# Row maxima sent by GpSimd's own DMA queue instead of SyncE's, and 80 unread products added on TensorE

## The reference, cut to what matters

```python
x = x + tanh(g_xattn[0]) * L0_xattn(layernorm(x), ctx, ...)      # context attention, 77 context rows
x = x + tanh(g_ffn[0])   * L0_ffn(layernorm(x), wg, w1, b1, w2, b2)
x = x + tanh(g_xattn[1]) * L1_xattn(layernorm(x), ctx, ...)
x = x + tanh(g_ffn[1])   * L1_ffn(layernorm(x), ...)

def L0_ffn(x, wg, w1, b1, w2, b2):      # 8 experts, the best 2 of each row, capacity 256
    scores = softmax(x @ wg); topv, topi = top_k(scores, 2)
    ...                                  # rows sent to experts, relu(x @ w1 + b1) @ w2 + b2, gathered
def L1_xattn(x, img, ...):               # first part: self-attention, 16 heads of 8
    q = heads(nx @ W_sq + b_sq); k = heads(nx @ W_sk + b_sk); v = heads(nx @ W_sv + b_sv)
    s = einsum('bhqd,bhkd->bhqk', q, k) * SCALE
    so = merge(einsum('bhqk,bhkd->bhqd', softmax(s), v)) @ W_so + b_so
    ...                                  # then cross-attention and a gelu network
```

## Time and profile before

| | |
|---|---|
| median of 3 runs | 457.8 us (456.64 to 464.91) |
| the profiled execution's own time | 453.76 us |
| its span, first to last instruction | 452.0 us |
| TensorE busy | 349.2 us, 77% of the span |
| VectorE, ScalarE, GpSimd busy | 261.5, 201.8, 114.1 us |
| mean granted clock of TensorE | 0.89 |

### The profile page before, as it was taken

How to read it: one execution, slowest core, us unless ns; L and a number is a source line. 1 busy time by engine, 2 the same in 40 slices (tenths; PEclk the granted TensorE clock), 3 DMA queues, 4 the chain that set the end, 5 groups by cost and what they waited for, 6 DMA issues and landing times.

```text
span 452.0 us, 6689 instructions
## 1 busy us (share of the span) xinstructions
PE 349.2 (77%) x2487; PEld 208.2 (46%) x2487; DVE 261.5 (58%) x661; ACT 201.8 (45%) x317; POOL 114.1 (25%) x155
## 2 busy tenths in 40 slices
PE   1897500998089899999999799987972899988980
PEld 0676400897043422333323376554562443677860
DVE  5435500233379988888830687536369937773435
ACT  2321300322050777667787488564723435664210
POOL 2000178155140618111110000010000055562232
PEclk9998555899569999999999899998885899899986
DMA  4599112111306765100000000003999367431222
GB/s 113 149 190 326 55 52 78 50 35 40 116 24 172 192 168 122 29 3 2 3 1 1 0 0 1 2 0 122 392 305 290 128 203 235 144 98 36 62 78 52
DMA packets 35877, 46.01 MB, mean 102 GB/s; under 512 B 4779, under 2 KB 21683, under 8 KB 35845
## 3 DMA queue, kind: packets, MB, share of 16 engines
q1 hardware_dynamic: 33156, 38.57, 30.0%
q0 software_dynamic: 2688, 7.02, 5.5%
HBM read 31.67 MB, written 13.78 MB: 101 GB/s over the span
## 4 chain that ended last, share of the span: by engine, by line
PE 55%; DVE 13%; issue 9%; DMA 8%; ACT 7%; POOL 6%; SPq 1%; POOLq 0%; DVEq 0%; ACTq 0%
PE ps L1413 9%; PE ps L1620 6%; PE ps L1606 6%; PE ps L1581 5%; PE ps L1589 3%; DMA R<-h_d,srow 3%; PE ps L1722 3%; PE ps L1531 3%; POOL disp_d L541 2%; PE ps L1877 2%; PE ps L1770 2%; PE ps L1543 2%; PE ps L1731 2%; POOL y_d L554 1%; PE ps L1906 1%
## 5 line engine op out<-in xcount | busy, mean ns | idle before, releaser
L1222 DVE TENSOR_REDUCE early<-ps 128x1 f32<-128x512 f32 x128 | 81.3, 684 | 9.7 <-PE ps L1581 6.4
L758 ACT ACTIVATE R<-ps 128x1024 f32<-128x1024 f32 x64 | 62.5, 1020 | 19.8 <-PE ps L1606 18.9
L1413 PE MATMUL ps<-ident,R 128*77 128x128 f32 (+1 forms) x224 | 35.4, 296 | 31.9 <-DMA R<-disp_d 24.8
L1413 PEld LDWEIGHTS ps<-ident,R 128*77 128x77 f32 (+1 forms) x224 | 26.6, 152 | 50.5 <-DMA R<-disp_d 25.2
L1581 PE MATMUL ps<-R 72*128 72x512 bf16 x112 | 38.1, 381 | 0.9 <-DVE early L1222 0.8
L1606 PE MATMUL ps<-R 75*128 75x512 bf16 x128 | 37.6, 379 | 1.1 <-DMA R<-R 0.8
L624 POOL DMA_INDIRECT R<-h_d,srow x16 | 16.3, 1021 | 78.2 <-DMA h_d<-ff 71.2
L1620 PE MATMUL ps<-R,vaug 128*9 128x512 f32 x256 | 33.5, 595 | 0.6 <-ACT R L758 0.6
L1188 DVE TENSOR_SCALAR R<-ps,vcol 128x256 f32<-128x256 f32 x16 | 7.0, 479 | 38.0 <-PE ps L1531 38.0
L1581 PEld LDWEIGHTS ps<-R 72*128 72x128 bf16 x112 | 10.8, 96 | 31.5 <-DVE early L1222 20.9
L541 POOL DMA_INDIRECT disp_d<-R,srow x16 | 15.9, 993 | 37.2 <-DVE srow L1134 32.7
(11 more groups left out here) (324 smaller groups left out, 688.4 us busy)
## 6 DMA issues: line engine op xcount, KB each, us to landing
R<-in_L_ffn_W_dram SPq DMA_DIRECT2D x1, 6144.0 KB, 19.7
h_d<-R SPq DMA_DIRECT2D x12, 256.0 KB, 2.8
q_d<-R SPq DMA_DIRECT2D x24, 96.0 KB, 1.9
R<-k_d SPq DMA_DIRECT2D x24, 96.0 KB
R<-q_d SPq DMA_DIRECT2D x8, 288.0 KB
R<-in_L_ffn_w_dram SPq DMA_DIRECT2D x1, 2048.0 KB, 16.3
h_d<-ff SPq DMA_DIRECT2D x6, 256.0 KB, 2.4
disp_d<-R SPq DMA_DIRECT2D x1, 1032.0 KB, 12.2
```

Of the source, the lines that this page charges most:

```text
L758: s.activation(probs[idx % 4], ps[:, 2 * (idx % 2):2 * (idx % 2) + 2, :].rearrange("p b t -> p (b t)"), ACT.Exp, scale=QK_SCALE).then_inc( ...
L1222: v.tensor_reduce(mcol[:, u, col:col + 1], bank(ring_bank("row", n)), AX.X, ALU.max).then_inc(s1_max, 1)
L1413: return m.transpose(dst, src, ident[0:k, 0:k])
```

## The change

SyncE no longer sends the maxima. GpSimd waits for its own split of unit `u` and issues the three transfers itself, as part of its loop over the units, ahead of whatever it does next. TensorE gets 12 products of 512 columns ahead of the transposes of the first routing, 64 ahead of the transposes of sequence 0, and 4 between these and sequence 0's projections. All go to PSUM bank 1, which is free at these places, and wait for nothing.

```diff
-            def load_max(u):
-
-                b, hg = u // HG, u % HG
-                sp.wait_ge(max_parts, u + 1)
-                if u >= 2:
-                    sp.wait_ge(ld_max[u % 2], 16 * 3 * (u // 2))
-                for i in range(3):
-                    sp.dma_start(Q9[KQ + i:KQ + 1 + i, b, 4 * hg:4 * hg + 4, :].rearrange("p h (t q) -> p (h t) q", q=P),
-                                 mparts[:, u, i, :]).then_inc(ld_max[u % 2], 16)
-
...
             load_packed(0, 2)
-            load_max(0)
             load_packed(0, 3)
...
-            load_max(1)
             load_packed(1, 0)
             load_packed(1, 1)
-            load_max(2)
             load_packed(1, 2)
             load_packed(1, 3)
-            for u in range(3, UNITS):
-                load_max(u)
...
                 g.tensor_tensor(mparts[:, u, 2, :], mneg[:, :], mparts[:, u, 1, :], ALU.subtract).then_inc(max_parts, 1)
+                pool.wait_ge(max_parts, u + 1)
+                if u >= 2:
+                    pool.wait_ge(ld_max[u % 2], 16 * 3 * (u // 2))
+                b, hg = u // HG, u % HG
+                for i in range(3):
+                    g.dma_start(Q9[KQ + i:KQ + 1 + i, b, 4 * hg:4 * hg + 4, :].rearrange("p h (t q) -> p (h t) q", q=P),
+                                mparts[:, u, i, :]).then_inc(ld_max[u % 2], 16)
                 if u == 0:
                     pool.wait_ge(qk_ready, K_1)
...
+            def spin(columns):
+
+                m.matmul(ps[:, 1, 0:columns], ones_b[:, :], zeros[:, 0:columns // 2].bitcast(BF16), start=True, stop=True)
+
...
+            for i in range(12):
+                spin(512)
             transpose_tiles(sent[0][:, :, 0:D], ln_out, T, ln_tp)
...
-            def spin(columns):
-
-                m.matmul(ps[:, 1, 0:columns], ones_b[:, :], zeros[:, 0:columns // 2].bitcast(BF16), start=True, stop=True)
-
+            for i in range(64):
+                spin(512)
             transpose_tiles(xn, ln_out, 2 * T, ln_tp, [0])
+            for i in range(4):
+                spin(512)
             project_heads(0, 0)
```

More of the change, by code:

```diff
@@ L458, in _ @@
             sp.wait_ge(q_parts, 2)
-            for hg in range(HG):
-                store_queries(1, hg)
-            load_max(1)
+            store_queries(1, 0)
+            store_queries(1, 1)
+            store_queries(1, 2)
+            store_queries(1, 3)
             load_packed(1, 0)
             load_packed(1, 1)
-            load_max(2)
             load_packed(1, 2)
             load_packed(1, 3)
-            for u in range(3, UNITS):
-                load_max(u)
             sp.wait_ge(o_norm, 4 * HG)
```

## The result

Over 21 runs of each kernel the median is 462.5 us with the change and 459.7 us before. The ratio is 1.0091, with a 95% interval of 1.0058 to 1.0124: under 2%, but a small loss all the same, 4.2 us (2.7 to 5.7). It leaves out every execution over 1.5% above the fastest of its kernel, so it is not the quotient of the two medians (1.006). The same kernel run again beside three others gave 1.0092 (1.0034 to 1.0149). The forecast was 0.7 us more.

What follows compares the result with a forecast made beforehand. TensorE bounds steady loop steps; its clock falls at the routing and sequence 0. The sum 453.76 - 1.8 - 0.9 + 3.4 = 454.5 us, 0.7 more, became 458.5 on the runs' median; own range 456.5 to 460, wide 453 to 465.

Steps and rivals of the forecast that it cites:

- 1.8 forecast: First routing: 12 products hold the clock through transposes and logits, so the first scatter comes 1.8 us earlier; bounds 0 to 2.3.
- its reserve: Sequence 0: the masked copy of Q waits on VectorE's variances at 129.89 us, so 1.07 us at best arrives.
- 0.3 gained for 0.9: Sequence 0: the 64 + 4 products were forecast to bring the first scores 0.9 us earlier.
- Three take 3 x 0.98 + 2 x 0.30 = 3.54 us: Attention loop: GpSimd's time to issue a unit's three transfers, 3.54 us, taken from its indirect transfers.
- The waits forecast for units 3 and 7: Attention loop: late maxima cost 1.3 us in unit 3 and 1.6 us in unit 7.
- the rival of cheap transfers: Attention loop: direct transfers cost GpSimd 0.6 to 0.9 us each, landing in 3.2 to 4.2; time 455.1 to 456; chance 0.30.
- Three ... land 4.77 us after the parts: Attention loop: each unit's maxima land 4.77 us after GpSimd's parts, against 5.26 us available in a steady step.
- named contention only as a bound: Attention loop: contention or a longer form appears only in the upper bound, 6.3 us to landing.
- taken as 3.18 us from unit 7: Attention loop: SyncE's way, from its start at 232.64 to the wait's end at 235.82 in unit 7, at most 3.18 us.
- The term was +3.4 us: Attention loop: moving transfers to GpSimd adds 3.4 us of waits, 0.5 + 1.3 + 1.6; 0 by SyncE's bound, 13 by the upper.
- waits in every unit: Rival, attention loop: maxima land 6.2 us after parts, steady units wait 0.94 us each, 13.4 together; time 468.5; chance 0.12.
- the wide range: Whole kernel: 453 to 465 us, the top set half way to the case of waits in all units.

Runs made afterwards that it cites:

- pool_only: The changed kernel without any unread products, maxima still sent by GpSimd; ratio to the kernel before 1.0126 (1.0072 to 1.0180).
- pool_guard2: The changed kernel, all products, with SyncE's packed loads held until the maxima of units 0, 1 and 2 land; ratio to before 0.9939 (0.9893 to 0.9986).
- guard2_bare: The changed kernel without unread products, SyncE's packed loads held behind the maxima of units 0, 1 and 2; ratio to before 0.9936 (0.9891 to 0.9980).
- after_again: The changed kernel itself, unaltered, run again for a comparison beside three others and a second trace; ratio to before 1.0092 (1.0034 to 1.0149).
- split_units: The changed kernel, but SyncE sends the maxima of units 0 and 1, GpSimd those of 2 to 7; ratio to before 1.0079 (1.0038 to 1.0120).
- pool_warm: The changed kernel plus 24 unread products, 16 ahead of unit 0's wait and 8 ahead of unit 1's; ratio to before 1.0033 (0.9987 to 1.0079).
- guard3: The changed kernel, packed loads held behind units 0, 1 and 2, load (0,2) too waiting for unit 0's maxima; ratio to before 0.9995 (0.9954 to 1.0036).
- sp_spins: The changed kernel with all products, but the maxima given back to SyncE at their old places; ratio to before 1.0004 (0.9964 to 1.0044).
- guard2_64: The changed kernel with only the 64 + 4 products, packed loads held behind units 0, 1 and 2; ratio to before 0.9992 (0.9949 to 1.0035).

## Why the time lay in the stated range and the steps did not hold

- **12 products.** The clock held at 42 to 44 us and the first scatter came 1.4 us earlier, for 1.8 forecast. The passes of the logits did not all run at full clock: in this trace it fell at about 44.4 (0.61 from 44 to 46), and L1480 took 2.83 us, not 1.9. The rule of the Trainium skill that was weighed here ("TensorE: Matmul & The Clock Gate", Part 4: transposes don't count as busy for the clock as other products do) fits this trace; in the first trace of the changed kernel L1480 took 1.90 us, at full clock, behind the same transposes, so it did not decide in every execution. Of the ten traces with the 12 products five have 1.90 us, one 2.2 and four 2.7 to 2.8.
- **64 + 4 products.** The forecast's rows were right (L1560 in 1.98 us), its reserve was too: the masked copy waits for VectorE's variance. But that variance slipped. GpSimd's split of K (L546) also started earlier, and beside it VectorE's 128x4 operation took 0.98 us in place of 0.17 a few microseconds before. From the first transpose to the first scores: 7.12 us before, 6.82 after, 0.3 gained for 0.9.
- **GpSimd's time for the transfers.** "Three take 3 x 0.98 + 2 x 0.30 = 3.54 us", from indirect rows: measured 1.48 to 1.59. The waits forecast for units 3 and 7 are not in the trace, or are 0.30 us; the rival of cheap transfers was right in its mechanism.
- **The step that failed.** "Three ... land 4.77 us after the parts", for each unit alike. The forecast counted GpSimd's time and a fixed way, named contention only as a bound, and read the diff's removal of `load_max(0)` from between two loads as nothing but a shorter queue. In the traces the landing follows the loads in flight: 8.2 us after the parts in unit 0 (147.07 + 0.41 to 155.68) and 8.0 in pool_only, where I had written 154.2 for parts at 149.4, and 4.9 in pool_guard2, where one load fewer stands in front. The trace of the kernel before already had the sign: SyncE's own transfers, taken as 3.18 us from unit 7, took 5.6 in unit 0, from 149.44 to 155.07. The term was +3.4 us, made of waits in units 1, 3 and 7; the transfers alone measured +5.8 (3.3 to 8.2), and the traces put it in unit 0 above all, a wait of over 3 us and the clock behind it.
- **The clock in the loop.** No step asked what a wait of 3 us does to the clock in a stage that the earlier trace rows shows at full clock; the rival "waits in every unit" priced a wait at its own length. Behind the wait of 3.37 us there were 6.8 at half clock.
- **The sum.** 0.7 us forecast, 4.2 measured (2.7 to 5.7). The time given, 458.5 us, is 4.0 below the median of 462.5; 1.9 of that is before's own median, 459.7 for the 457.8 shown. The measured time is above the forecast's own range of 456.5 to 460. It lies in the wide range only because that went half way up to "waits in every unit", a rival that did not come true: that is luck. Two errors had opposite signs: the products gained less than 2.7 us, and the transfers lost more than 3.4, while their issue was cheaper.

What stays open: why pool_guard2 and guard2_bare are 0.6% faster than before while three neighbours of them are level with it. The intervals of 0.4 to 0.5% each would allow all five to be 0.3% faster. Also how the gain ahead of the loop is lost again. Two traces offer one way, each of them a single execution: after_again, whose clock fell in the loop, kept it in stretches behind the loop in which pool_guard2's fell. After_again, then pool_guard2:

```profile
252.00:256.00 4.00, 2.55 (x20) 2.12 (x19) 3.00 (x14) 2.07 (x3) 0.00 (x0) 1.00 0.01 4
256.00:260.00 4.00, 2.32 (x7) 0.95 (x7) 3.59 (x17) 1.67 (x3) 0.00 (x0) 1.00 0.00 0
...
316.00:320.00 4.00, 3.13 (x17) 1.94 (x16) 2.72 (x13) 1.64 (x3) 0.00 (x0) 1.00 0.89 289
```

```profile
252.00:256.00 4.00, 2.88 (x6) 1.03 (x6) 3.54 (x14) 1.79 (x4) 0.00 (x0) 0.60 0.00 0
256.00:260.00 4.00, 3.81 (x7) 2.18 (x8) 0.00 (x0) 1.81 (x3) 0.00 (x0) 0.55 0.00 0
...
316.00:320.00 4.00, 4.00 (x6) 1.40 (x5) 3.66 (x8) 2.79 (x4) 0.00 (x0) 0.50 1.05 406
```

pool_guard2 left the loop at 241.7 and after_again at 247.5, but their spans are 452.3 and 452.2 us. It is no rule: between 250 and 350 us the clock was at half for 12 us in after_again and 29 in pool_guard2, but for 30 in split_units, whose clock had fallen in the loop for 10. No kernel tested this.

## What to carry to other kernels

A small transfer moved to another engine's queue also leaves its place among the large transfers: before you price its issue, list which loads will be in flight when it is issued, and if it is urgent, hold them behind it with a wait on the queue that sends them. A guard must cover every urgent transfer that follows, or the late landing only moves to the next one. And price a wait of TensorE in a stage at full clock with the half clock that may come behind it: here up to 3.4 us on a wait of 3.4, of which pool_warm won back 1.2 (its trace) to 2.7 (the times, not clear of noise).

## What the runs showed of the hardware that was not expected

- Three direct transfers of 16 x 128 values cost GpSimd 1.48 to 1.59 us, about 0.5 each, where its indirect ones take 0.98; SyncE takes 1.77 for the same three.
- Such a transfer lands 1.5 to 1.6 us after its issue on quiet DMA engines (the lower end and the median in after_again, as below; their busy share was 0.01 from 190 to 245 us) and 6.7 us after it behind three packed loads.

```profile
DMA to landing us min/median/max: 1.5/1.6/6.7
```

- A VectorE operation on 128x4 elements took 0.98 us when it started 0.2 us behind GpSimd's 128x512 operation (L966 and L546 above), and ended with it; it took 0.17 us where the two did not meet (before, pool_only, guard2_bare).
- After a wait of 3.37 us the clock was still full when TensorE resumed and fell about 1.4 us later. Shorter waits were followed by half clock too: 0.66 us in guard3, 1.31 in sp_spins, 1.54 in guard2_bare; one of 1.36 us in guard2_64 was not.
